# Local attention: even and odd heads on the two row halves, one projection bank, two transposes in one bank

## What is computed

```python
def attn_layer(x, Wqkv, qs, ksc, Wo):            # HEADS 16, DIM_HEAD 64, WINDOW 32
    q, k, v = split(x @ Wqkv)                     # 16 heads of 64
    q = l2norm(q) * qs
    k = l2norm(k) * ksc
    q = q * cos * scale + rotate_half(q) * sin * scale
    k = k * cos / scale + rotate_half(k) * sin / scale
    out = local_attention(q, k, v)                # each query sees the 32 keys before it and itself
    return out @ Wo

for i in range(DEPTH):                            # 6
    x = attn_layer(shift_tokens(x), Wqkv[i], q_scale[i], k_scale[i], Wo[i]) + x
    x = ffn_layer(shift_tokens(x), ln_g[i], ln_b[i], W1[i], b1[i], W2[i], b2[i]) + x
```

## Time and profile before

| | us |
|---|---|
| median of 3 runs (lowest, highest) | 4648.19 (4643.84, 4649.11) |
| the profiled execution, its own time | 4650.33 |
| its span, first to last instruction | 4648.5 |
| TensorE busy in the span | 4341.6 (93%) |
| VectorE, ScalarE, GpSimd busy | 3854.4, 3635.1, 3383.3 |

### The profile page before, as it was taken

How to read it: one execution, slowest core, us unless ns; L and a number is a source line. 1 busy time by engine, 2 the same in 40 slices (tenths; PEclk the granted TensorE clock), 3 DMA queues, 4 the chain that set the end, 5 groups by cost and what they waited for, 6 DMA issues and landing times.

```text
span 4648.5 us, 135499 instructions
## 1 busy us (share of the span) xinstructions
PE 4341.6 (93%) x47296; PEld 3494.1 (75%) x47296; DVE 3854.4 (83%) x9773; ACT 3635.1 (78%) x11591; POOL 3383.3 (73%) x2447
## 2 busy tenths in 40 slices
PE   7988869999889999889999799998899998899997
PEld 5666647888768888678888678887688886788886
DVE  7988878888778888778888688887788887788886
ACT  6889967888748888658888478887488886588884
POOL 4544448888658888568888388886588885688882
PEclk9999989999989999989999999999899999899998
DMA  2000000000000000000000000000000000000000
GB/s 76 0 0 1 0 14 2 0 0 0 6 20 1 0 0 0 6 20 0 0 0 1 24 2 0 0 0 6 19 1 0 0 0 6 6 0 0 0 1 19
DMA packets 31380, 26.63 MB, mean 6 GB/s; under 512 B 10308, under 2 KB 23490, under 8 KB 31170
## 3 DMA queue, kind: packets, MB, share of 16 engines
q1 hardware_dynamic: 31170, 23.96, 1.8%
HBM read 21.85 MB, written 2.10 MB: 5 GB/s over the span
## 4 chain that ended last, share of the span: by engine, by line
PE 75%; DVE 12%; issue 7%; ACT 3%; POOL 2%; DVEq 0%; SPq 0%; DMA 0%; ACTq 0%; POOLq 0%
PE bank L659 17%; PE bank L706 13%; PE bank L754 10%; PE bank L732 9%; PE bank L652 7%; PE bank L717 7%; PE bank L820 4%; PE bank L692 4%; DVE top L1270 3%; PE bank L834 2%; DVE qk_parts L1245 2%; PE bank L635 1%; DVE qk_t L1406 1%; DVE by_sin L1238 1%; ACT prob L888 1%
## 5 line engine op out<-in xcount | busy, mean ns | idle before, releaser
L1070 POOL TENSOR_TENSOR rotated<-by_cos,by_sin 128x512 f32<-128x512 f32 x768 | 981.4, 1278 | 394.6 <-DVE by_sin L1320 377.3
L1078 POOL TENSOR_TENSOR rnorm<-norm2g,neg_half 128x16 f32<-128x16 f32 x384 | 1115.5, 2905 | 163.7 <-DVE norm2g L1333 163.7
L963 ACT ACTIVATE bank<-bank,top 128x128 f32<-128x128 f32 x3072 | 1064.1, 352 | 10.9 <-DVE top L1340 4.0
L1090 POOL TENSOR_TENSOR rotated<-rotated,rnorm 128x512 f32<-128x512 f32 x768 | 786.5, 1047 | 0.5
L1312 DVE TENSOR_TENSOR by_cos<-bank,rot_cos 128x512 f32<-128x512 f32 x768 | 531.2, 692 | 256.9 <-PE bank L659 248.6
L945 ACT ACTIVATE qk_t<-bank 128x512 f32<-128x512 f32 x768 | 459.9, 599 | 286.5 <-PE bank L652 285.9
L706 PEld LDWEIGHTS bank<-qk_t 64*64 64x64 f32 x12288 | 529.2, 133 | 193.0 <-issue 193.0
L706 PE MATMUL bank<-qk_t 64*64 64x64 f32 (+1 forms) x12288 | 674.2, 237 | 0.0
L963 ACT ACTIVATION_READ_ACCUMULATOR bank<-bank,top 128x1 f32 x3072 | 669.4, 218 | 0.0
L659 PE MATMUL bank<-wqkv_high,xt_high 128*128 128x512 f32 (+1 forms) x1536 | 598.6, 390 | 11.0 <-ACT vout L974 11.0
L1320 DVE TENSOR_TENSOR by_sin<-bank,rot_sin 128x256 f32<-128x256 f32 x1536 | 572.9, 415 | 0.0
(11 more groups left out here) (148 smaller groups left out, 8904.1 us busy)
## 6 DMA issues: line engine op xcount, KB each, us to landing
wqkv_sb<-in_L_ffn_Wqkv_dram SPq DMA_DIRECT2D x36, 256.0 KB, 4.1
wo_sb<-in_L_ffn_Wo_dram SPq DMA_DIRECT2D x48, 64.0 KB, 2.0
out_dram<-y SPq DMA_DIRECT2D x8, 256.0 KB, 3.5
w_sb<-in_L_ffn_W_dram SPq DMA_DIRECT2D x6, 341.0 KB, 3.0
w_sb<-in_L_ffn_W_dram SPq DMA_DIRECT2D x12, 64.0 KB
cst<-in_constants_dram SPq DMA_DIRECT2D x1, 518.0 KB, 3.5
b_sb<-in_L_ffn_b_dram SPq DMA_DIRECT2D x1, 384.0 KB
w_sb<-in_L_ffn_W_dram SPq DMA_DIRECT2D x6, 42.5 KB
```

The costliest lines, as they stand in the source:

```text
L963: last = nc.scalar.activation(at, at, ACT.Exp, bias=top[jl % 2][:, h:h + 1], accum_out=psum_raw[jl % 2][:, h:h + 1])
L1070: nc.gpsimd.tensor_tensor(rotated[j % 4][:, :, :, :], by_cos[j % 2][:, :, :, :], by_sin[j % 2][:, :, :, :], ALU.add).then_inc(c_rot, 1)
L1078: nc.gpsimd.tensor_tensor(rnorm[slot][:, :, :].rearrange("t g n -> t (g n)"), norm2g[slot][:, :, :].rearrange("t g n -> t (g n)"), neg_hal ...
L1090: nc.gpsimd.tensor_tensor(at, at, rnorm[slot][:, i, :].unsqueeze(2).to_broadcast([P, 2 * HG, DH]), ALU.mult).then_inc(c_unit, 1)
```

## The change

* Scores: a step scores the four heads of one group. Even heads are on rows 0 to 63 and odd heads on rows 64 to 127 of the same `qk_t`; their products alternate, and each row half writes into a bank of its own. `win_ps` names the two pairs of banks (4 and 5, 1 and 2) that consecutive groups take in turn.
* Mask: four bf16 products of 64 x 64 pieces with 256 columns each, on the same quarters of the array as the scores, in place of one fp32r product of 512 columns. The waits in front of it go.
* Projection: one bank (bank 0) in place of two, so the projection of group j waits for the squares of group j-1 (`c_sq, g`).
* Transposes: the probabilities' go into bank 3, which the heads' use too. The head transposes wait for the copy of the step's earlier probability transposes (`c_pt`), the probability transposes for the copy of this step's heads (`c_qk`).
* Order: TensorE transposes heads right behind the scores; ScalarE copies them right behind the squares, ahead of the values; VectorE takes the maxima right behind the scaling, ahead of the norms.
* The heads' order in `value_ps` and the rows of `wo_sb` follow, with as many DMAs as before; the constant `band` is twice as wide.

```diff
-        proj_ps = bank[0:2]
+        win_ps = [t[:, :].rearrange("q (e n) -> q e n", e=2)[:, :, 0:2 * P] for t in (pair45, pair12)]
+        proj_ps = bank[0]
         misc_ps = bank[2]
-        turn_c_ps = bank[2]
+        turn_c_ps = bank[3]
...
-                for u in range(2):
-                    for jj in range(HG):
-                        sp.dma_start(wo_sb[PAD * jj:PAD * (jj + 1), u * NG * P:(u + 1) * NG * P].rearrange("r (s c) -> r s c", s=NG),
-                                     wo[l].rearrange("(u j s r) c -> u j r s c", u=2, j=HG, r=PAD)[u, jj]).then_inc(s_wo_in, 16)
+                for h in range(HG):
+                    for half in range(2):
+                        sp.dma_start(wo_sb[PAD * h:PAD * (h + 1), :].rearrange("r (g s c) -> r g s c", g=NG, s=2)[:, :, half, :],
+                                     wo[l].rearrange("(g h s r) c -> h s r g c", g=NG, h=HG, r=PAD)[h, half]).then_inc(s_wo_in, 16)
...
             def win_heads(layer, it, j):
-                    if has(it * STEPS + j - WIN.turn - 1):
+                    if has(it * STEPS + j - 1 - WIN.probs):
+                        pe.wait_ge(c_pt, g + WIN.turn - WIN.probs)
+                    elif has(it * STEPS + j - WIN.turn - 1):
                         pe.wait_ge(c_qk, g)
...
             def win_project(layer, it, j):
-                    if has(it * STEPS + j - 2):
-                        pe.wait_ge(c_sq, g - 1)
+                    if has(it * STEPS + j - 1):
+                        pe.wait_ge(c_sq, g)
...
             def win_mask(layer, it, j):
-                    m = layer * GROUPS + it * STEPS + j - WIN.scores
-                    if (j - WIN.scores) % 2 == 0:
-                        pe.wait_ge(c_qk, m + 2)
-                    if has(it * STEPS + j - WIN.scores - 2):
-                        pe.wait_ge(c_scaled, m - 1)
-                    nc.tensor.matmul(score_ps[(j - WIN.scores) % 2][:, :].rearrange("q (h k) -> q h k", h=HG), ident_r[:, :],
-                                     band_r[:, :].unsqueeze(1).to_broadcast([P, HG, P]), start=True, stop=False,
-                                     skip_group_check=True)
+                    for half in range(2):
+                        for e in range(2):
+                            rows, lower = slice(e * DH, (e + 1) * DH), half * DH
+                            nc.tensor.matmul(win_ps[(j - WIN.scores) % 2][lower:lower + DH, e, :].rearrange("q (i k) -> q i k", i=2),
+                                             ident_b[rows, rows], band_b[rows, half, :].unsqueeze(1).to_broadcast([DH, 2, P]),
+                                             start=True, stop=False, skip_group_check=True, tile_position=(e * DH, lower))
...
             def win_scores(layer, it, j):
-                    for jj in range(HG):
-                        src = qk_t[(jl - e) % 4 + jj // 2]
+                    for i in range(2):
                         for lower, keys in ((0, slice(0, DH)), (DH, slice(WINDOW, P))):
-                            q0, k0 = (jj % 2) * P + lower, (2 + jj % 2) * P
-                            last = nc.tensor.matmul(score_ps[e][lower:lower + DH, jj * P + keys.start:jj * P + keys.stop], src[rows, q0:q0 + DH],
-                                                    src[rows, k0 + keys.start:k0 + keys.stop], start=False, stop=False,
-                                                    skip_group_check=True, tile_position=(e * DH, lower))
+                            for e in range(2):
+                                rows, q0, k0 = slice(e * DH, (e + 1) * DH), i * P + lower, (2 + i) * P
+                                last = nc.tensor.matmul(win_ps[jl % 2][lower:lower + DH, e, i * P + keys.start:i * P + keys.stop],
+                                                        qk_t[jl % 4][rows, q0:q0 + DH], qk_t[jl % 4][rows, k0 + keys.start:k0 + keys.stop],
+                                                        start=False, stop=False, skip_group_check=True, tile_position=(e * DH, lower))
...
             def win_turn_probs(layer, it, j):
+                    if here(it, j, WIN.turn):
+                        pe.wait_ge(c_qk, layer * GROUPS + it * STEPS + j - WIN.turn + 1)
                     pe.wait_ge(c_scaled, m + 1)
...
             def win_step(layer, it, j):               # TensorE
                 win_scores(layer, it, j)
+                win_heads(layer, it, j)
                 win_sum_values(layer, it, j)
                 win_project_out(layer, it, j)
                 win_turn_next(layer, it, j)
-                win_heads(layer, it, j)
                 win_turn_probs(layer, it, j)
...
             def win_step(layer, it, j):               # ScalarE
                 win_square(layer, it, j)
+                win_copy_heads(layer, it, j)
                 win_copy_values(layer, it, j)
                 win_copy_next(layer, it, j)
-                win_copy_heads(layer, it, j)
                 win_copy_probs(layer, it, j)
...
             def win_step(layer, it, j):               # VectorE
                 win_scale(layer, it, j)
+                win_max(layer, it, j)
                 win_norms(layer, it, j)
                 win_tok_next(layer, it, j)
-                win_max(layer, it, j)
```

More of the change, by code:

```diff
@@ L84 @@
 for _name, _n in (("ident", P), ("shift", P), ("iota", P), ("qrow", P), ("split", 8), ("block", HG), ("cos", 2 * DH),
-                  ("sin", 2 * DH), ("causal", P), ("band", P)):
+                  ("sin", 2 * DH), ("causal", P), ("band", 2 * P)):
     COLS[_name] = (_at, _n)
@@ L130, in constants @@
     put("causal", np.where(ahead >= 0, 0.0, MASKED))
-    put("band", np.where((ahead >= 0) & (ahead <= WINDOW), 0.0, MASKED))
+    band = np.where((ahead >= 0) & (ahead <= WINDOW), 0.0, MASKED)
+    put("band", np.concatenate([np.tile(band[lower:lower + DH], (2, 1)) for lower in (0, DH)], 1))
     return t
@@ L162, in build @@
         causal_b = sb("causal_b", [P, P], BF16)
-        ident_r = sb("ident_r", [P, P], F32R)
-        band_r = sb("band_r", [P, P], F32R)
+        band_b = sb("band_b", [P, 2, P], BF16)
         neg_half = sb("neg_half", [P, 4 * HG])
@@ L241, in build, with ps @@
         hidden = [flat(b) for b in by_cos + by_sin + rotated[0:2]]
-        bank = [stack.enter_context(nc.psum_tensor(f"bank{i}", [P, 512], F32)) for i in range(8)]
-        proj_ps = bank[0:2]
+        def ps(name, banks=1):
+            return stack.enter_context(nc.psum_tensor(name, [P, banks * 512], F32))
+        bank0, pair12, bank3, pair45, bank6, bank7 = ps("bank0"), ps("pair12", 2), ps("bank3"), ps("pair45", 2), ps("bank6"), ps("bank7")
+        bank = [bank0, pair12[:, 0:512], pair12[:, 512:1024], bank3, pair45[:, 0:512], pair45[:, 512:1024], bank6, bank7]
+        win_ps = [t[:, :].rearrange("q (e n) -> q e n", e=2)[:, :, 0:2 * P] for t in (pair45, pair12)]
+        proj_ps = bank[0]
         misc_ps = bank[2]
-        turn_c_ps = bank[2]
+        turn_c_ps = bank[3]
         acc_ps = bank[6]
@@ L680, in win_values @@
                         pe.wait_ge(c_vout, layer * VOUTS + it * STEPS + j)
+                    if isinstance(it, int) and 0 <= it * STEPS + j - WIN.scores < 2:
+                        pe.wait_ge(c_qk, layer * GROUPS + it * STEPS + j - WIN.scores + 1)
                     gc = (j % NG) * HG * DH
@@ L727, in win_sum_values @@
                     pe.wait_ge(c_pt, m + 1)
-                    e = jl % 2
                     for half in range(2):
-                        for jj in range(HG):
-                            at = 2 * P + (2 * (jj % 2) + e) * DH + half * PAD
-                            last = nc.tensor.matmul(value_ps[PAD * jj:PAD * (jj + 1), half * P:(half + 1) * P],
-                                                    vout[jl - e + jj // 2][:, at:at + PAD], prob_t[jl % 2][:, jj, :],
-                                                    start=True, stop=True, tile_position=(0, PAD * jj))
+                        for h in range(HG):
+                            at = 2 * P + h * DH + half * PAD
+                            last = nc.tensor.matmul(value_ps[PAD * h:PAD * (h + 1), half * P:(half + 1) * P],
+                                                    vout[jl][:, at:at + PAD], prob_t[jl % 2][:, h % 2 * 2 + h // 2, :],
+                                                    start=True, stop=True, tile_position=(0, PAD * h))
                     last.then_inc(c_value, 1)
@@ L953, in win_square @@
                         act.wait_ge(c_nrm2, g)
-                    nc.scalar.activation(squares[:, :, :].rearrange("t h d -> t (h d)"), proj_ps[j % 2][:, :], ACT.Square).then_inc(c_sq, 1)
+                    nc.scalar.activation(squares[:, :, :].rearrange("t h d -> t (h d)"), proj_ps[:, :], ACT.Square).then_inc(c_sq, 1)
             def win_exponentials(layer, it, j):
@@ L961, in win_exponentials @@
                     for h in range(HG):
-                        at = score_ps[jl % 2][:, h * P:(h + 1) * P]
```

(11 more changed lines are left out.)

11 lines of the change are left out of this document (4 added, 7 removed).

## The result

| | before | after |
|---|---|---|
| median of 4 runs each | 4648.65 us | 4527.06 us |
| lowest, highest | 4643.84, 4649.27 | 4525.86, 4527.32 |
| span of the profiled execution | 4648.5 us | 4525.2 us |

The ratio is 0.9739, 95% interval 0.9727 to 0.9752: 122 us less, where 153 were forecast. The time lies in the stated range and 32 us above the forecast.

What follows compares the result with a forecast made beforehand. TensorE was taken to set the pace, with two chains of waits next. A group falls 0.90 us, x 177 = 159: 4650.3 - 159 + 6 = 4497, less 2 for profiling, 4495 us; range 4380 to 4640.

Steps and rivals of the forecast that it cites:

- TensorE's piece: Mask, scores and shape changes in TensorE's step: quarters side by side, 0.41 us saved, plain step 3.78 us.
- Chain 1: Probability transposes wait for ScalarE's head copy, which stands behind the squares: no plain step below 3.9 us.
- Chain 2: Path through VectorE's norms and GpSimd's scaled heads: TensorE waits 0.2 us before head transposes every second step.
- The group: Four attention steps, one sequence: 16.36 us in place of 17.26, 0.90 less, 159 us over 177 groups.
- Start of a layer: Second projection waits for the first squares, 3.0 us against 2.1: 1 us a layer, 6 us more in all.
- What was priced at nothing: Output weights' order and DMAs, fewer casts at the start, maximum and scale over two banks: no cost.
- row halves take turns: Rival, slower: row halves of mask and scores alternate, 4684 us, or about 5180 us all in series; 15%.
- all of TensorE's saving arrives: Rival: both chains shorter and VectorE without a stall, 15.62 us a group, 4364 us; 9%.
- The longer chain 1: Rival: squares to head copy takes 0.67 us, not 0.48, near 4580 us; gain gone at 4640 to 4657, 6%.
- The signs: Profile after: scores 0.35, mask 0.12, group 16.4 us, TensorE waits for head copy and GpSimd, clock 1.00, VectorE near 93%.

Runs made afterwards that it cites:

- e3: Changed kernel with ScalarE's head copy ahead of the squares and the head transposes one step later: 4430.21 us.
- e8: Changed kernel with the four mask products issued twice: 4527.66 us.
- e5: Changed kernel with the score products of all even heads issued first, then all odd ones, instead of alternating: 4527.43 us.
- e4: e3 with TensorE's head transposes also moved ahead of the mask, so three changes of tile shape a step, not four: 4384.48 us.
- e9: e4 with ScalarE's squares put back ahead of the head copy: 4474.08 us.
- e2: Changed kernel with the head transposes one step later (lag 4 instead of 3): 4488.49 us.
- e7: Kernel before the change with a single projection bank, so a projection waits for the squares of the step before: 4656.36 us.
- e1: Changed kernel with ScalarE copying the transposed heads ahead of the squares: 4527.25 us.

## Why the prediction was right, and where it was off

*TensorE's piece.* The four quarters side by side: right, 0.08 us a pass in each. From the last value pass to the head transposes the forecast had 0.09 + 0.12 + 0.33 + 0.09, and the trace has 0.09 + 0.13 + 0.43, 0.02 more. The added fourth change of shape was put at 0.09 and cost 0.15 (heads to values 0.59 in place of 0.44). So TensorE's own plain step is 3.85 (e3), not 3.78: a term off by 0.07, which by itself moved nothing in the changed kernel, where e8 adds 0.11 more for nothing.

*Chain 1.* Forecast 3.87, rounded to 3.9; the faster groups have 3.91 to 3.94, the slower 3.98 to 3.99. By terms: 0.98 and 2.37 as forecast, 0.49 for 0.48, copy 0.59 for 0.60, waking TensorE (put at 0.06) 0.05 or, in the slower groups, 0.13 (copies ending at 1025.10, 1029.09, 1033.13, transposes at 1025.23, 1029.22, 1033.26), transposes to projection 0.41 or 0.42 for 0.36, since a first pass that has waited takes longer (in the step shown 0.17 up to the second pass, and 0.11 in e5, where it hasn't). That it sets the pace is shown by e8 (TensorE has time to spare) and by the pair e4 and e9 (taken away and put back, with 90 us between them). Why it is 0.05 in one group and 0.13 in the other stays open.

*Chain 2.* Forecast a wait of 0.2 us in the sequence step; the trace has 0.17 to 0.27 more between scores and heads there than elsewhere, and e2 takes it away for 39 us. The sequence step of 4.55 to 4.65 is TensorE's own 4.37 (e2) plus that wait; the forecast was 3.78 + 0.51 = 4.29 plus 0.2.

*The group.* 16.49 for 16.36. This is the term that was mis-sized: 0.76 saved a group for 0.90. Over the 28 groups or so behind step 16 in each layer that is 0.13 x 28 x 6, some 22 of the missing 32 us. The forecast's four steps were 3.9, 4.08 (VectorE with the token copy), 3.9 and 4.49; the slower groups have 3.99, 4.05, 3.98, 4.55, the faster ones 3.92, 3.94, 3.91, 4.65. So what is missing is 0.08 or 0.09 in each plain step of the slower groups and 0.06 to 0.16 in the sequence step, less the 0.14 by which the token step of the faster groups came out shorter than VectorE's 4.08. That the average lies so near the forecast is in part these signs cancelling.

*Start of a layer.* The first eight steps take 1.5 us longer than before, forecast 1 us, 3 us more in six layers. The mechanism is right, and e7 shows it alone. The two paces behind the forecast were both too short, 3.0 us a step for 3.72 and 2.1 for 2.83 to 3.02: they came from rows of the body at a clock of 1.00, and here it is 0.50. That their difference came out near is luck.

*What was priced at nothing.* From the last projected group of a layer to the first of the next it takes 118.4 to 119.8 us, before 118.05 to 118.57: about 1 us a layer. In six layers that is some 6 us more, which with the 22 and the 3 above leaves 1 of the missing 32. The windows of the MLP stretch of the first layer show a granted clock of 0.86 where the kernel before, here in the first row, had 0.89; both lie between the two levels, so the engine spends part of the stretch at the lower:

```profile
1262.47:1356.32 93.85, 73.23 (x425) 58.82 (x426) 63.94 (x175) 31.54 (x47) 34.77 (x30) 0.89 0.10 29
1239.69:1335.29 95.60, 75.18 (x426) 60.30 (x426) 63.95 (x175) 31.48 (x46) 34.78 (x30) 0.86 0.10 29
```

TensorE is busy for 18.8 us of the 24.2 in the drain ahead of it, 20.6 before, and there the clock is 0.97 or 0.98 where it was 1.00 in four layers of five. Over five layers the MLP stretch has 0.84 to 0.88, before 0.88 to 0.89; where both kernels have 0.88, the whole stretch takes 118.44 and 118.57 us, the same. But the layer with the lowest clock, 0.84, takes 118.98, less than the three with 0.86 (119.4 to 119.8). I had said that the clock stays at 1.00 in the body, which it did, and hadn't looked at the stage behind it. That the clock is the cause is read from these windows and not shown: no experiment was made for it.

*Rivals.* That row halves take turns is refuted by the trace, and by e5 even for an order that invites it. That all of TensorE's saving arrives needed both chains gone, and e3 is that kernel, at 4430 us. The longer chain 1 didn't come in the way that was priced (squares to head copy 0.49, not 0.67); the slower groups show some of it, by the 0.13. The signs: pieces, group and clock came as stated, TensorE's wait for the head copy is smaller (plain steps of 3.91 to 3.99 on a TensorE that needs 3.85, so 0.06 to 0.14 for 0.1 to 0.2), its wait for GpSimd comes once in four steps, and VectorE is busy for 361.9 of 400 us, 90% and not 93%. As for the Trainium skill, its rule that changing the tiling mode drains TensorE (TensorEngine Tiling, Key Properties) agrees with e4, where one change fewer took 0.15 us from TensorE's step, and its statement that different tiles multiply in parallel agrees with the 0.08 us above.

## What to carry to other kernels

When three engines stand at 86% behind the one that sets the pace, write down each loop of waits through one step, with the durations of the rows, before believing in the bound engine's saving; here TensorE's sum promised 1.64 us a group, 0.76 arrived, and shortening the two loops by an edit of one line each (e3) made it 1.31 and took another 97 us off the kernel's time. An addition that costs nothing (the mask twice, 84 us of TensorE's time, 0 us of the kernel's) shows at once that an engine at 99% busy isn't the bound. And edits that shorten one of two nearly equal loops can measure as nothing: e1 alone brought 0 us, on top of e2 58.

## What the runs showed that I had not expected

* TensorE overlaps the two row halves even when all products of one half are queued ahead of the other's: scores 0.49 us against 0.43 when they alternate.
* What a change of tile shape costs depends on what stands on both sides of it. The same head transposes take 0.44 us when transposes of their own shape follow, 0.53 when the 64 x 64 mask follows (e4) and 0.59 when the values' products on 128 rows and 32 columns do: 0.09 and 0.15.
* In the version with both chains shortened and three shape changes (4384.48 us, 5.7% below the kernel before, the fastest here), VectorE, busy for 374.8 of 400 us, is the engine to look at first; that it is the bound wasn't tested.
